# Two-layer graph network on one core: the combination of expert results and the second projection as one stage

## What is computed

```python
# end of layer 0: top-2 mixture of 16 experts, residual, layer norm
moe = jnp.sum(topk_w[..., None] * sel, axis=2)        # sel: the two experts' rows
y = x + moe
ffn0 = (y - mu) / jnp.sqrt(var + EPS) * gamma + beta  # EPS = 1e-5
# between the layers: the result is added to x and x is layer-normalised; rows r
# start of layer 1, two branches from the same rows
x_lin = (r @ W).reshape(N, H, C)                      # graph attention, 4 heads
a_src = jnp.einsum('nhc,hc->nh', x_lin, att_src)      # and a_dst alike
qkv = rmsnorm(r, w_norm1) @ w_qkv                     # linear attention, 8 heads
q = elu(q) + 1.0; k = elu(k) + 1.0                    # = max(z, 0) + exp(min(z, 0))
kv = einsum('bnhd,bnhm->bhdm', k, v); ksum = k.sum(axis=1)
```

## Time and profile before

| | |
|---|---|
| median of 3 runs | 2919.01 us (2914.56 to 2919.16) |
| the profiled execution's own time | 2919.62 us |
| its span in the profile | 2917.9 us |
| mean granted TensorE clock | 0.765 |
| PE, DVE, POOL, ACT busy | 58%, 63%, 62%, 29% of the span |
| stage_combine | about 1625 to 1725 us of the span |
| stage_project1 | about 1725 to 1912 us |
| stage_edges1, its gathers | 1919.8 to 2549.6 us |

### The profile page before, as it was taken

The page is one execution under the profiler, slowest core; times in us unless marked ns, Lnnn a source line. Parts: engine busy times, 40 slices in busy tenths (PEclk is TensorE's granted clock), DMA queues, the critical chain, the costliest instruction groups (busy, mean ns, idle before and its releaser), DMA issues. The chain is left out here.

```text
span 2917.9 us, 53010 instructions
## 1 busy us (share of the span) xinstructions
PE 1684.7 (58%) x12561; PEld 1225.7 (42%) x12562; DVE 1836.3 (63%) x5583; ACT 839.3 (29%) x2657; POOL 1813.5 (62%) x1828
## 2 busy tenths in 40 slices
PE   0487444146666665408999228845666655401897
PEld 0254333034444444405666116624555544401565
DVE  8776799477777777502222562268888887776322
ACT  0244111034444444102333133313333333311221
POOL 3777777767777776777775537657777777700000
PEclk9998666578888887558999658867766676655899
DMA  7010000063333333052333300033333337321000
GB/s 220 10 22 18 2 2 1 2 211 106 107 107 106 106 107 85 1 207 80 85 86 85 114 24 21 20 88 106 105 104 106 105 105 151 103 51 57 26 14 21
DMA packets 169723, 224.46 MB, mean 77 GB/s; under 512 B 77731, under 2 KB 129226, under 8 KB 169513
## 3 DMA queue, kind: packets, MB, share of 16 engines
q0 software_dynamic: 74368, 138.96, 17.7%
q1 hardware_dynamic: 95270, 84.55, 10.1%
HBM read 184.08 MB, written 39.29 MB: 77 GB/s over the span
## 5 line engine op out<-in xcount | busy, mean ns | idle before, releaser
L2137 POOL DMA_INDIRECT e_rows<-mid_table,e_rec x488 | 481.4, 986 | 185.2 <-issue 138.6
L244 POOL DMA_INDIRECT mid_sorted<-p_record,p_row x391 | 416.5, 1065 | 160.0 <-issue 122.5
L921 POOL DMA_INDIRECT e_rows<-mid_table,e_rec x440 | 420.2, 955 | 150.7 <-issue 88.6
L244 POOL DMA_INDIRECT mid_sorted<-keep_record,keep_row x391 | 395.3, 1011 | 127.0 <-issue 119.0
L1083 PE MATMUL e_ps_A<-e_rows,e_hot 128*125 128x260 f32 x880 | 311.5, 487 | 0.0
L1083 PEld LDWEIGHTS e_ps_A<-e_rows,e_hot 128*125 128x125 f32 x880 | 191.0, 241 | 25.7
L2394 ACT ACTIVATE e_acc<-e_state 128x66 f32 x488 | 126.1, 258 | 251.7 <-ACT e_acc L2394 212.0
L1068 PE MATMUL e_ps_T<-e_identb,e_hot 128*125 128x128 bf16 x446 | 85.8, 283 | 179.5 <-DVE e_hot L944 177.7
L2459 PE MATMUL e_ps_mT<-keep_ident,e_marked 128*128 128x128 f32 x488 | 117.8, 422 | 123.3 <-DVE e_marked L2161 123.3
L1442 DVE COPY x_hidden<-x_ps_h 128x512 f32<-128x512 f32 x64 | 44.3, 692 | 222.8 <-PE x_ps_h L1471 222.8
L2459 PEld LDWEIGHTS e_ps_mT<-keep_ident,e_marked 128*128 128x128 f32 x488 | 95.1, 222 | 134.6 <-issue 134.6
(11 more groups left out here) (532 smaller groups left out, 4086.1 us busy)
## 6 DMA issues: line engine op xcount, KB each, us to landing
e_rows<-mid_table,e_rec POOLq DMA_INDIRECT x928, 2.7
mid_expert_in<-p_zrow SPq DMA_DIRECT2D x1, 8192.0 KB
w<-in_L_ffn_w SPq DMA_DIRECT2D x16, 512.0 KB
x_w<-in_L_ffn_w SPq DMA_DIRECT2D x16, 512.0 KB
x_xs<-mid_expert_in SPq DMA_DIRECT2D x64, 128.0 KB
x_b<-in_L_ffn_b SPq DMA_DIRECT2D x64, 128.0 KB
mid_expert_out<-x_y SPq DMA_DIRECT2D x64, 128.0 KB
mid_sorted<-p_record,p_row POOLq DMA_INDIRECT x391
```

What stands on the lines that cost most here:

```text
L244: pool.indirect_dma_start(out=to, out_offset=bass.IndirectOffsetOnAxis(ap=row[:, t:t + 1].bitcast(U32), axis=0), in_=record[:, t, :], in_o ...
L921: pool.indirect_dma_start(out=rows[:, s % RING * 2 + j, :], out_offset=None, in_=k["table"], in_offset=bass.IndirectOffsetOnAxis(ap=rec[:, ...
L2137: pool.indirect_dma_start(out=rows[:, j, q, :], out_offset=None, in_=k["table1"], in_offset=bass.IndirectOffsetOnAxis(ap=rec[:, i * TG + q ...
```

## The change

Both stages become one, `stage_project1`, with one block. While PE projects a group, DVE and ACT combine the next one between the tiles of the projection. Beside that:

- The two norms are made at once: ACT takes one root of 10 columns (`two_roots`), the rows are written with the product of both factors, and `xn` goes. `edges1` multiplies the stored rows by `rms` again where it adds them to the mix (`add_mix`).
- max(z, 0) is no longer an ACT instruction: one `scalar_tensor_tensor` of DVE makes max(z, 0) + exp straight from PSUM, for queries and keys.
- The score weights are 8 more columns of the graph weights, and a column of ones stands in the values, so that L1929 and L1901 go. ACT scales the scores tile by tile.
- The graph bias is added in turns 53 to 57 of `stage_edges1`.
- `SCATTERS_EARLY` is 300: 30 record scatters move from the projection to the experts.
- Index load, cast and clearing of the sums (`sums1`) move from the start of `stage_edges1` to the end of the new stage.
- The loops over groups are written out, and the big buffers of the two stages share memory (`room`).

The cut of the record scatters:

```diff
-SCATTERS_EARLY = 270
+SCATTERS_EARLY = 300
```

ACT in the new stage (`keep_tile` is L1790, the scores, L1796 and L1794 of before for one tile; `normalise` writes the rows of a group):

```diff
+            def project(u):
+                act.wait_ge(s_xT, u + 1)
                 keep_transposed(nc.scalar, s_xTk, xT[:], ps_T)
+                act.wait_ge(s_lowq, u + 1)
+                nc.scalar.activation(lowq[:], lowq[:], ACT.Exp).then_inc(s_expq, 1)
+                for j, t in enumerate(columns(u)):
...
+                    keep_tile(t, j)
+                    if j == 1 and u + 1 < NB:
+                        root(u + 1)
+                    if j == 3 and u + 1 < NB:
+                        two_roots(u + 1)
+                if u + 1 < NB:
+                    normalise(u + 1)
```

DVE (`weigh`, `measure_y`, `centre_y`, `add_y`, `measure_x`, `spread_of_x` and `scales` are the steps of `take`, `add` and `scales` of before, cut into pieces; `low_part` is L1836), and its end:

```diff
+            def key_of(t, j):
+                dve.wait_ge(s_exp, t + 1)
+                v.scalar_tensor_tensor(key[:, j, :], ps_p[0:NP, t % 2, 0:D], 0.0, low[:, j, :], ALU.max, ALU.add).then_inc(s_k, 1)
+
+            def project(u):
+                n = u + 1
+                more = n < NB
+                dve.wait_ge(s_q, n)
+                for bank, at, size in SPANS:
+                    last = v.tensor_scalar(lowq[:, at:at + size], ps_T[:, bank, 0:size], 0.0, None, ALU.min)
+                last.then_inc(s_lowq, 1)
+                if more:
+                    weigh(n, 0)
...
+                low_part(t, 0)
+                dve.wait_ge(s_expq, n)
...
+                last.then_inc(s_qT, 1)
+                key_of(t, 0)
+                if more:
+                    weigh(n, 1)
+                low_part(t + 1, 1)
+                if more:
+                    measure_y(n)
+                key_of(t + 1, 1)
+                low_part(t + 2, 2)
+                if more:
+                    centre_y(n)
+                key_of(t + 2, 2)
+                if more:
+                    add_y(n)
+                low_part(t + 3, 3)
+                if more:
+                    measure_x(n)
+                key_of(t + 3, 3)
+                if more:
+                    spread_of_x(n)
+                low_part(t + 4, 4)
+                if more:
+                    scales(n)
+                key_of(t + 4, 4)
...
+            o.done(v.memset(k["sums1"], 0.0))
+            dve.wait_ge(s_rec, 16)
+            o.done(v.tensor_copy(k["rec"][:, 0:G1_N, 0].bitcast(I32), k["rec"][:, 0:G1_N, 0]))
```

PE (`state` adds a tile's key times value):

```diff
+            def turn(u):
+                pe.wait_ge(s_xn, u + 1)
+                if u:
+                    pe.wait_ge(s_qT, u)
...
+            for u in range(NB):
+                turn(u)
+                if u:
+                    state(u * TB - 1)
+                queries(u)
+                for j, t in enumerate(columns(u)):
+                    if t >= 2:
+                        pe.wait_ge(s_k, t - 1)
                     for c in range(DC):
+                        last = mm(ps_p[0:NP, t % 2, :], xT[:, j, c, :], w[:, c, D:3 * D], start=c == 0, stop=c == DC - 1)
                     last.then_inc(s_qk, 1)
...
+                        last = mm(ps_v[0:NP, t % 2, 0:D + 2 * H], xT[:, j, c, :], w[:, c, 3 * D:], start=c == 0, stop=c == DC - 1)
                     last.then_inc(s_vx, 1)
+                    if j:
+                        state(t - 1)
```

Taken out of POOL, and of DVE, at the start of `stage_edges1`:

```diff
-            pool.wait_ge(s_idx, 1)
...
-            o.done(v.memset(acc[:], 0.0))
-            dve.wait_ge(s_rec, 16)
-            v.tensor_copy(index, rec[:, 0:G1_N, 0]).then_inc(s_idx, 1)
```

546 lines of the change are left out of this document (239 added, 307 removed).

## The result

The changed kernel takes **2842.31 us**, the median of 4 runs (2839.42 to 2852.14); the kernel before, run beside it, 2919.09 (2914.56 to 2919.37). The profiled execution took 2843.54 us, its span is 2841.8.

What follows compares the result with a forecast made beforehand. Combination was taken as bound by DVE, projection by PE, edges by POOL. From 2919.6 us, 54.9 for earlier scores and 6.7 for the edges' earlier start gave 2858.0 us; range 2846 to 2884.

Steps and rivals of the forecast that it cites:

- the ring: New stage: DVE waits for a group's queries before combining the next group, whose rows the next queries need; 37.8 us a group.
- one group, 37.8 us: New stage, from one group's queries to the next: DVE, ACT's last tile and rows, transposes, keeping and queries take 37.8 us.
- the term of the queries, 7.3: PE's query products in each group of the new stage: 7.3 us, kept from before with the clock at 0.50.
- DVE ready at 21.7: Within a group, DVE has the next group's factors 21.7 us behind the queries: 21.2 of work, 0.5 for handovers.
- 6.7 us for index, clearing and cast: Start of the edges: first gather 0.7 instead of 7.4 us behind the first DMA, saving 6.7 us.
- Rival 3: Start of the edges: DVE's preparation or the gap before the first turn eats the 6.7 us; 2865 us, chance 0.07.
- The bias adds: Edge turns 53 to 57: each add at most 2.1 us where DVE idles 2.2; costs nothing while POOL bounds.
- POOL in the experts, 4.8 us left: End of the experts: 30 moved scatters take 38.4 of POOL's 43.2 idle us, leaving 4.8; costs nothing.
- rival 4: Experts: POOL's scatters finish late or slow the loads; at worst all 38 us show, 2896 us, chance 0.04.
- low clock in the tiles: Projection tiles: PE waits for keys and the clock stays at 0.50; 46 us a group, 2907 us, chance 0.08.
- Tables dear: ACT stands still around each table load as long again, 1.3 us each for two a group; 2868 us, chance 0.05.
- Lockstep: Tiles at the low clock: DVE's waits on PE and ACT double to 26 us a group; 2962 us, chance 0.03.

Runs made afterwards that it cites:

- the third group: Four kernels, among them the changed one, on a chip where every kernel takes longer: kernel before 4133.23 us, changed kernel 4060.34 us, ratio 0.9826.
- The kernel with the combination apart: Changed kernel, but all five groups are combined and their rows written first, then the projection runs with no combination in it: 2849.81 us, ratio 0.977.

## Why the prediction missed

The direction, the ring and its order were right; the sizes weren't. The failed step is **one group, 37.8 us**, measured 34.1, and in it above all the term of the queries, 7.3, measured 5.5. The terms:

- *DVE ready at 21.7*: 20.3. The pieces overlap a little more than 21.2 + 0.5 allowed; that is 1.4 us. The low part and the new form that reads PSUM took 0.42, as taken.
- *ACT's last tile and the rows*: 24.8 instead of 26.2, the 1.4 us of DVE; the 2.5 of the tile and the 2.6 of the rows were right. *Transposes 2.4*: 2.35. *Keeping 1.6*: 1.4.
- *Queries 7.3, "I keep that"*: 4.5 and 6.5 in turn, 5.5 on average. This is the largest part, 1.8 us. I took a duration that belongs to what ran before it, a pause of PE, for one that belongs to the instruction. Two readings went with it: 7.30 is the longest of the five in the kernel before (7.0 on average), and the 0.50 of the earlier trace rows is the clock of the queries' first 3.7 us only, over all 6.6 of them it was 0.67.

Four steps make 14.9 us. That alone is more than the 12 us that the range had below the forecast. The range had named this very cause, at up to 3 us in five groups, which is 15 us and more than the 12 that it allowed. The rest:

- *First queries*: 49.4 us behind SP's first DMA, 50.2 by the forecast, 0.9 less; the queries in it took 6.5, not 7.3. *Last group 17.4*: 16.1. *Scores 2.5*: 3.2, the first of their two waits for PE is 1.11 us instead of 0.37. *SP's 11.4*: 11.5.
- *6.7 us for index, clearing and cast*: 6.6 when undone. Rival 3 is refuted.
- *The bias adds, "nothing, as long as POOL bounds"*: 4.3 us of the 4.7 by which the gathers take longer. That sentence looked at DVE's slack only. The adds hold up POOL's gathers, and POOL is what bounds; DVE's slack is no cover for that. The last gather was forecast at about 2488 and came at 2470.7. Of the turns 53 to 57 three begin without a wait for rows, so this sign failed as well.
- *POOL in the experts, 4.8 us left*: 0.5, and 1.1 us of the end is POOL's. Small, but the reserve was misread; of rival 4's 38 us that much came. It is part of the term *ahead of the new stage* below.
- *Behind the last gather*: 1.8 us more. Not examined, its cause is open.
- *Ahead of the new stage*: 4.7 us less in the profiled execution, though the code there is the same but for the 30 scatters. The range had no term for what unchanged stages do from run to run. These 4.7 us are why the time fell below the range at all: with them back it would be some 2847, just inside. On which side of the border it fell is chance; the 3.7 us of each group are not.

Together, for the profiled execution: 2858.0 - 14.9 - 0.9 - 1.3 + 0.7 + 0.1 - 4.7 + 4.7 + 1.8 = 2843.5, measured 2843.54. The two misses that go the other way, adds and tail, hid part of the error.

The rivals: *low clock in the tiles* came for one tile in each of the first four groups. The first products of the fourth tile take 2.9 to 3.2 us instead of 1.88, behind a wait of 1.9 us for a key; DVE doesn't wait for it, so it costs the ring nothing. *Tables dear*: a load takes 1.28 us, and the exponential starts 0.01 us behind it; ahead of it there is no gap either. The 1.38 us of drain beside each load that the Trainium skill states ("ScalarE: Activation LUTs", What ACT_TABLE_LOAD costs) don't show here, and the 11 us that followed from it didn't come. *Lockstep*: DVE waits 2 us in a group, not 26.

And one thing the forecast had right for a reason it didn't see. It set the merged ring of 37.8 us against 14.2 + 35, as if the gain were the overlap. The kernel with the combination apart shows 15.2 + 21.8 = 37.0 against 34.1. Most of the gain of this change is the projection's own step, from 35 to 21.8, 13 us in each of four steps. Of these, 3.6 are transposes and queries at the full clock (5.7 us instead of 9.3), and a pause put back cost 5.6, its own length and the same clock together. How the rest divides among the folded products, the bias add and the scaling that are gone, and the sum and maximum in one instruction, no run here shows.

## What to carry to other kernels

Before two stages are laid over each other, ask what each would take alone after the same cleaning; here the kernel with both apart, but cleaned, lost only 8 of the 77 us. In a ring, put what does not depend on the awaited result ahead of the wait: one such move gave 10 us, and with the rest of the pieces, the adds and the stores moved as well 26. And work placed in the slack of one engine has to be checked against the engine that bounds: a DVE add of 1.49 us cost POOL's gather 0.83 to 0.90. A duration read in one place carries over only with what ran before it: the queries took 4.5 to 7.3 us in these traces.

## What the hardware showed that was not expected

- A matmul's time at the start of a group depends on PE's pause before it. The same 16 products of the queries took 4.49 us at a granted clock of 1.00 behind full work, 6.2 to 6.4 at 0.70 behind three waits of 3.5 us in sum, 6.6 to 7.3 at 0.60 to 0.67 in the kernel before. In the changed kernel about 4.5 and 6.5 alternate from group to group in both its traces outside the third group.
- POOL's indirect gather that starts 0.2 to 1.1 us into a DVE instruction with two inputs in SBUF (1.23 or 1.49 us long) ends 0.81 to 0.83 us behind it, 62 times out of 62. Two that started in the same moment as such an instruction took their usual 0.94.
- One chip gave 4133 us for the kernel whose medians on the chips of the other groups are 2917 to 2921, with unchanged durations on DVE, a lower granted clock on PE, and idle gaps of 8 to 19 us between DVE's instructions, which in the ring stand in the first step only. What it lacks the traces don't say.
